# GpSimd in place of VectorE adds the high and low halves of the state behind span 3

## The reference, cut to what matters

```python
h = relu(einsum('ts,bsh->bth', adj, x @ Wg0 + bg0))
h = relu(einsum('ts,bsh->bth', adj, h @ Wg1 + bg1))
for p in range(1, 5):                       # spans 1 to 4
    nw = T // p
    wins = h[:, :nw * p].reshape(B * nw, p, H)
    last = lstm_last(Wih[p-1], Whh[p-1], ..., wins)   # p steps in a row
    h = h.at[:, arange(nw) * p + (p - 1)].set(last)   # the last node of each window
x = layernorm(x + h)
```

## Time and profile before

| | |
|---|---|
| median of 3 runs | 1026.88 us (1026.53 to 1027.72) |
| the profiled execution, its own time | 1026.49 us |
| its span in the profile | 1024.7 us |
| PE busy | 993.9 us, 97% |
| DVE busy | 571.5 us, 56% |
| ACT busy | 374.7 us, 37% |
| POOL busy | 19.8 us, 2% |
| mean granted TensorE clock | 0.99 of full speed |

### The profile page before, as it was taken

One profiled execution on the slowest core, in us unless ns is written; L12 is line 12 of the kernel. 1 busy time (PEld: TensorE's weight loads), 2 busy tenths in 40 slices (PEclk: granted clock), 3 DMA queues, 4 the chain that ended last, 5 costly groups with the idle time before them and its releaser, 6 DMA issues.

```text
span 1024.7 us, 14363 instructions
## 1 busy us (share of the span) xinstructions
PE 993.9 (97%) x5386; PEld 867.1 (85%) x5386; DVE 571.5 (56%) x1357; ACT 374.7 (37%) x680; POOL 19.8 (2%) x22
## 2 busy tenths in 40 slices
PE   8999999999999999999999999999999999999882
PEld 6888998889988899888897889898989889889882
DVE  7242353323443234332486556877686777877887
ACT  7231111221112220222334444555464544646551
POOL 0000000000000000000000000101010100100000
PEclk9999999999999999999999999999999999999897
DMA  9400000000000000000220000000000000000001
GB/s 313 135 1 0 1 1 1 1 1 1 1 0 0 0 0 0 0 0 0 82 82 1 1 1 2 0 2 21 1 1 21 0 21 0 21 5 17 1 21 42
DMA packets 21919, 20.42 MB, mean 20 GB/s; under 512 B 1008, under 2 KB 18544, under 8 KB 21872
## 3 DMA queue, kind: packets, MB, share of 16 engines
q1 hardware_dynamic: 21872, 19.81, 6.1%
HBM read 15.61 MB, written 4.19 MB: 19 GB/s over the span
## 4 chain that ended last, share of the span: by engine, by line
PE 91%; DVE 6%; ACT 1%; DMA 1%; issue 0%; SPq 0%; DVEq 0%; ACTq 0%
PE ps L593 27%; PE ps L594 27%; PE ps L595 27%; PE ps L742 9%; DMA square<-in_adj_t 1%; PE ps L633 1%; PE ps L921 1%; ACT gates_last L1052 0%; DVE gates_last L1396 0%; PE ps L762 0%; DVE xb L1172 0%; DVE stats L1129 0%; ACT gates_last L1062 0%; DVE xb L1474 0%; DVE gates L1396 0%
## 5 line engine op out<-in xcount | busy, mean ns | idle before, releaser
L593 PE MATMUL ps<-adj,node 128*128 128x512 f32 x368 | 144.7, 393 | 3.2 <-DVE adj L1112 1.9
L594 PE MATMUL ps<-adj,node 128*128 128x512 f32 x368 | 143.5, 390 | 0.0
L595 PE MATMUL ps<-adj,node 128*128 128x512 f32 x368 | 143.5, 390 | 0.0
L1112 DVE TENSOR_TENSOR y<-ps,y 128x512 fp32r<-128x512 f32 x46 | 31.8, 692 | 174.1 <-ACT y L984 174.1
L984 ACT ACTIVATE y<-ps 128x512 fp32r<-128x512 f32 x46 | 27.5, 598 | 271.8 <-PE ps L595 271.7
L593 PE MATMUL ps<-adj,h 128*128 128x512 f32 x256 | 99.7, 389 | 0.0
L594 PE MATMUL ps<-adj,h 128*128 128x512 f32 x256 | 99.7, 389 | 0.0
L595 PE MATMUL ps<-adj,h 128*128 128x512 f32 x256 | 99.6, 389 | 0.0
L1115 DVE SCALAR_TENSOR_TENSOR h<-ps,h 128x512 fp32r<-128x512 f32 x112 | 76.4, 689 | 40.2 <-ACT h L984 39.4
L742 PE MATMUL ps<-s,adj 128*128 128x256 f32 x768 | 93.7, 283 | 0.0
L742 PEld LDWEIGHTS ps<-s,adj 128*128 128x128 f32 x768 | 92.9, 192 | 0.3
(11 more groups left out here) (233 smaller groups left out, 1981.7 us busy)
## 6 DMA issues: line engine op xcount, KB each, us to landing
adj_raw<-in_adj_t SPq DMA_DIRECT2D x8, 512.0 KB, 6.9
square<-in_adj_t SPq DMA_DIRECT2D x7, 512.0 KB, 8.5
out<-xb SPq DMA_DIRECT2D x7, 512.0 KB, 3.2
xb<-in_x SPq DMA_DIRECT2D x6, 512.0 KB, 8.0
lw_raw<-in_wih_t SPq DMA_DIRECT2D x1, 1024.0 KB, 5.6
xb<-in_x SPq DMA_DIRECT2D x2, 384.0 KB, 7.2
lw_raw<-in_whh_t SPq DMA_DIRECT2D x1, 768.0 KB, 7.1
square<-in_adj_t SPq DMA_DIRECT2D x2, 256.0 KB, 3.2
```

The source lines that it names most:

```text
L593: pe.matmul(dst, stat(HI), mov(HI), start=start, stop=False)
L594: pe.matmul(dst, stat(HI), mov(LO), start=False, stop=False)
L595: return pe.matmul(dst, stat(LO), mov(HI), start=False, stop=stop)
L1112: nc.vector.tensor_tensor(dst, src, f32(hi), ALU.subtract).then_inc(done, 1)
```

## The change

The eight additions into `hfull` move from DVE to GpSimd. GpSimd's loop over slots now walks the steps of a slot in order: at the step where the copies of the even nodes stood it makes them as before, and at (3, 2) it waits for `h_done` of that step and for the transposes that read `hfull` in earlier slots, and makes the addition. Since DVE's order no longer covers it, DVE waits for `open_set` of the batch before ahead of its write of the odd nodes to `hw`, GpSimd does so ahead of its copies, and the second group of transposes waits for `open_set` as the first one did.

```diff
@@ GpSimd
-            back = 1
-            for slot in range(back, SLOTS):
...
+            def set_open(slot, back):
+
+                hi, lo = (f32(runs_in(slot, back)[:, i, :]).rearrange(
+                    "q (a b v) -> q b a v", a=PER_BLOCK, v=PITCH)[:, 0:BLOCKS - 1, :, 0:RUN] for i in (HI, LO))
+                nc.gpsimd.tensor_tensor(full_in(slot, back)[:].rearrange(
+                    "q (b v a) -> q b a v", b=BLOCKS, a=PER_BLOCK)[:, 0:BLOCKS - 1], hi, lo,
+                    ALU.add).then_inc(open_set, 1)
+
+            for slot in range(1, SLOTS):
+                steps = steps_of(slot)
+                runs_at = max(k for k, u in enumerate(steps) if u.p == 1)
+                if slot - 1 < B - 2:
+                    runs_at = max([runs_at] + [k for k, u in enumerate(steps) if (u.p, u.s) == (SKIPS, 2)])
+                for k, u in enumerate(steps):
+                    if k == runs_at:
+                        if slot - 1 == B - 2:
+                            pool.wait_ge(out_early, 16 * OUT_BEFORE_LATE)
+                        pool.wait_ge(h_done, AHEAD["unit"][slot] + k + 1)
+                        if 1 < slot < B - 1:
+                            pool.wait_ge(open_set, slot - 1)
+                        set_runs(slot, 1)
+                    if (u.p, u.s) == (3, 2):
+                        pool.wait_ge(h_done, AHEAD["unit"][slot] + k + 1)
+                        if AHEAD["fin"][slot] > 0:
+
+                            pool.wait_ge(fin_mm, AHEAD["fin"][slot])
+                        set_open(slot, u.back)
@@ PE, ahead of the transposes
-                        if t1 <= OPEN_TILES:
-                            pe.wait_ge(open_set, batch_of(slot, turn, back) + 1)
-                        else:
+                        pe.wait_ge(open_set, batch_of(slot, turn, back) + 1)
+                        if t1 > OPEN_TILES:
@@ DVE, ahead of the odd nodes
                             elif v.p == 2:
+                                if 0 < slot - v.back < B - 2:
+
+                                    dve.wait_ge(open_set, batch_of(slot, turn, v.back))
@@ DVE, behind (3, 2)
-                            if (v.p, v.s) == (3, 2):
-
-                                dve.wait_ge(h_done, ahead("unit", slot, turn, n_ended))
-                                hi, lo = (f32(runs_in(slot, v.back)[:, i, :]).rearrange(
...
-                                nc.vector.tensor_tensor(full_in(slot, v.back)[:].rearrange(
...
-                                    ALU.add).then_inc(open_set, 1)
```

More of the change, by code:

```diff
@@ L572, in _, with set_runs @@
                                     base=0, pattern=[[-1, P]], channel_multiplier=1).then_inc(eye_set, 1)
-            back = 1
-            for slot in range(back, SLOTS):
[L576 to L582, removed]
+            def set_runs(slot, back):
                 of, to = h_in(slot, back), runs_in(slot, back)
@@ L1416, in dve_slot @@
                             n_cell += 2
-                            if (v.p, v.s) == (3, 2):
-                                dve.wait_ge(h_done, ahead("unit", slot, turn, n_ended))
-                                hi, lo = (f32(runs_in(slot, v.back)[:, i, :]).rearrange(
-                                    "q (a b v) -> q b a v", a=PER_BLOCK, v=PITCH)[:, 0:BLOCKS - 1, :, 0:RUN]
-                                    for i in (HI, LO))
-                                nc.vector.tensor_tensor(full_in(slot, v.back)[:].rearrange(
-                                    "q (b v a) -> q b a v", b=BLOCKS, a=PER_BLOCK)[:, 0:BLOCKS - 1], hi, lo,
-                                    ALU.add).then_inc(open_set, 1)
                         continue
```

## The result

The changed kernel takes 1029.95 us (median of 8 executions, 1028.03 to 1030.46) against 1026.7 before (8, 1026.4 to 1027.72) on the same chip: ratio 1.0027, 95% interval 1.0018 to 1.0036. It is slower, by 3.25 us where 1.04 was forecast, and outside the range.

What follows compares the result with a forecast made beforehand. PE was taken to bound the slots, the last batches' chain of gates, ACT, DVE and PE the last slot. Slots 0, batch 6 0.44 and batch 7 0.60 made 1.04 us slower: 1027.9 us on the median, range 1025.2 to 1029.3.

Steps and rivals of the forecast that it cites:

- What bounds the kernel: PE, fully busy, bounds the loop's slots; the chain of gates, ACT, DVE and PE of the last batches bounds the last slot.
- The six additions in the slots: Additions of batches 0 to 5, 1.20 us each on DVE: moving them costs 0, covered by PE's full occupation.
- GpSimd's time: One addition of 774 elements a partition on GpSimd takes 1.83 us, between bounds of 1.25 and 2.41 us.
- The stops: In the last slot GpSimd's addition stops DVE's two-SBUF-input instructions and SBUF copies throughout, at two places: 0.44 and 0.60 us.
- Batch 6: Last slot, near 957.5 us: GpSimd lets a DVE instruction through, then its addition stops DVE's copy; 0.44 us later.
- Batch 7: Last slot, near 988.5 us: GpSimd gets in first and stops DVE's next two-input instruction; 0.60 us later, through to the end.
- the sum: Both last-slot delays reach the kernel's end in full: 0.44 + 0.60 = 1.04 us slower.
- the two gaps of 3 us that were there: PE's last-slot gaps of 3.05 and 3.20 us: the clock was low behind the first, 1.00 behind the second; either could change.
- The rival of the clock that falls once more: Clock falls in PE's second long last-slot gap, slowing the 12 matmuls behind it by 1.2 us: 1029.1 us, chance 0.10.
- The range: Whole kernel: 1025.2 to 1029.3 us, meant to hold each rival alone and leave out their doubles.

Runs made afterwards that it cites:

- g1: Changed kernel with the additions of batches 6 and 7 held back on GpSimd until DVE begins the layer norm's statistics, no fillers: 1026.01 us, ratio 0.9988.
- e4: The changed kernel run again with no edit: 1028.8 us, ratio 1.0013 to the kernel before.
- h3: Changed kernel with only batch 7's addition on GpSimd, the others back on DVE, no fillers: 1027.84 us, ratio 1.0017 to the kernel before.
- h1: Kernel with all PE gaps filled by identity transposes and, of the last slot's two additions, only batch 6's on GpSimd: 1025.4 us, ratio 0.9984.
- g2: Changed kernel with the additions of batches 6 and 7 held back until DVE's statistics, and all PE gaps filled by identity transposes: 1025.06 us, ratio 0.9981.

## Why the prediction was wrong

**What bounds the kernel** held. The six additions in the slots (0 forecast) measured nothing, and the second line of the table of places is equal to 0.01 us.

**GpSimd's time** held: 1.87 us for 1.83. The Trainium skill's estimate of 1.70 us (GPSIMD Engine Reference, section 3.1 Elementwise) was 0.17 too low for this strided addition. That 1.83 came so close is partly luck: it was the middle between two bounds, 1.25 and 2.41 us.

**The stops** held in kind and size. Batch 6: the order was as forecast (L1416 first, then GpSimd, then the copy), 0.36 us for 0.44. Batch 7: GpSimd got in first, 0.69 us for 0.60. Together they are 1.05 in the first profile and 1.10 with the clock held up, for 1.04. The rule of the Trainium skill (SBUF — State Buffer, section Who interferes with whom) agrees with what the traces show: two-input instructions and the copy wait for all of GpSimd's, and the statistics with one input don't.

**The step that failed is the sum,** where the delay of batch 7 "goes through in full" and nothing is added for what PE does in the longer wait. I saw that the clock can fall behind a gap and priced it, but only for the two gaps of 3 us that were there; the gap of 1.08 us, which my own step makes 0.6 longer, had no row and no chance of its own. At 1.80 us the clock fell behind it in the profiled execution, which cost 1.46 us, more than both stops together. In the low group are 13 of the changed kernel's 19 executions and 1 of 122 of the kernel before, and the two groups of the changed kernel lie 2.0 us apart (1029.51 and 1027.53). Those 2.0 us may hold other falls than this one, since the mean clock counts them all. The 1027.5 us of the rest are inside the range and 0.6 us over the rest of the kernel before.

The rival of the clock that falls once more (0.10, 1029.1 us) was meant for the last gap. There the clock was low too in the first profile, and the twelve matmuls took 1.18 us longer, for 1.2 in the forecast. But only 0.38 of it reached the end, because DVE was busy with the small operations of the layer norm until 1012.24. So its place was right and its price on the chain was wrong; the dear fall was at a gap that I hadn't named.

**The range** was too narrow for these reasons and for another: I took the clock and the start as things that one profile shows. The kernel before had 1026.4 to 1027.72 in the first eight executions and 1025.24 to 1030.15 over 122. How far off the forecast looks is in part a draw as well: the first eight executions gave 1029.95 us, the next eleven 1028.8. The difference of 3.25 us also isn't all accounted for: the late start is a draw in the profile, but how many of the eight executions had it isn't known.

## What to carry to other kernels

Where an engine waits for a chain of others, an added delay has two prices: its length, and what TensorE loses if the longer wait brings its clock down. List every gap that a change lengthens, not only the long ones. An addition moved from DVE to GpSimd can stop DVE for all of GpSimd's longer time. Here it stopped two-input instructions and a copy (one input isn't enough to be safe) and left the statistics alone; place it beside such work. And where executions differ by their granted clock, compare all of them by it, look in traces where the low stretches lie, and hold the clock up in both kernels when a difference of 1 us is to be seen.

## What the runs showed of the hardware

A gap of PE of 1.76 to 1.98 us in the last slot was followed by the lower clock (0.50) for 3.4 us in two of five traces, and one of 1.11 us or less at the same place in none of eleven. By mean clock 26 of 53 executions with the longer gap are in the low group, 1 of 122 of the kernel before, 0 of 22 with the longer gap partly filled, and 2 of 11 of g1.

The first gap of 3 us in the last slot was followed by 6.8 us at the lower level in the trace before, by 3.4 in eight others, and by none in those of e4 and h3. A short wait can stand ahead of a fall as well: in h3's trace the clock is 0.50 from about 8.4 to 11.8 us, near the kernel's start, and PE's wait ahead of that was 0.67 us.

Transposes of the identity, 0.12 us each, held the clock up in the last slot. With all gaps filled the mean clock was 0.993 to 0.996 in all 55 executions of five kernels, and the spread fell from 2.7 to about 1 us for four of them (2.1 for h1). At the start they weren't always enough: g2's trace is at 0.50 there for 3.4 us.

An addition of 774 elements a partition with strided operands takes 1.87 us on GpSimd and 1.20 on DVE. A copy of DVE's that met it took 1.99 us and a two-input instruction 1.94; both ended about 0.28 us behind GpSimd's end.
